# An attention and feed-forward kernel on one core: reciprocal ahead on VectorE, weight chunks over sixteen steps, transfers from SyncE, two banks for the down projection

## The chip, the cores and the metric

The kernel runs on one core of one Trainium2 chip. The metric is the device time of an execution in microseconds. Each core has TensorE (PE: matrix products into the eight banks of PSUM; PEld is its weight load), VectorE (DVE), ScalarE (ACT), GpSimd (POOL) and SyncE (SP, which here only issues transfers). Each engine executes its own instructions in the order of the program and waits at semaphores for the others.

## The reference

The input is x with 16 batches of 256 tokens and 256 features, all in float32. Two layers follow each other, each as x + layernorm(f(layernorm(x))):

```python
# attention, 16 heads of 128
q = (x @ Wq.T).reshape(b, n, 16, 128)
kv, kv_head, g = x @ Wkv.T, x @ Wkvh.T, x @ Wg.T
log_f_cumsum = cumsum(concat([0, log_sigmoid(g)]), axis=1)[:, :-1]
kv_head = cumsum(kv_head * exp(log_f_cumsum), axis=1)
k = einsum('bnd,bnh->bnhd', kv[..., :128], kv_head[..., :16])
v = einsum('bnd,bnh->bnhd', kv[..., 128:], kv_head[..., 16:])
q, k = rope(q), rope(k)
o = softmax(causal(q @ k / sqrt(128))) @ v;  out = o @ Wout.T
# feed forward
gate, up = split(x @ ternary_quant(w_gate_up).T)          # 2 x 1024
h = rms_norm(silu(gate) * up);  out = h @ ternary_quant(w_proj).T
```

ternary_quant works in bfloat16: a group of 64 weights has the scale mean(|w|), each weight is rounded to -1, 0 or 1 times it, and the result is w + (rounded - w).

## The kernel before

**Attention** goes over 16 batches, each in eight steps of two heads (a "pair"), 128 steps in all. The steps are software-pipelined by hand: the table `LAG` says how many steps after the projection of a pair (L725) a stage of it comes: cosine multiply on VectorE (`queries_cos`, L1273) and swap of halves on ScalarE (`swap`, L969) in the same step, sine multiply and addition on POOL one step later (L519, L528), the scores on TensorE (L742) and their maxima on VectorE (L1283) also one step later, softmax two (exponentials on ScalarE L981, `invert_sums`, the reciprocal of the sums, on VectorE L1299, `normalise` on POOL L550), transposition on TensorE three (L758) with its split into a high and a low part on ScalarE (L996) and VectorE (L1308), the product with the values four, the output projection five. Float32 products are three passes over high and low parts.

Work that comes once per batch lies in single steps by the tables `FRONT` (for the next batch) and `TAIL` (for the one before): layernorm statistics and normalisation of x (`stats_x`, `norm_x`, steps 0 and 1, VectorE, with `invert_x` on POOL), keys and gates (steps 3 and 4), decay and prefix sums (`decays` at the end of step 4, `coefs` and `sum_kv` in step 5), values (5 and 6), the copy of the attention's output and its layernorm (`copy_y` 5, `stats_y` 6, `norm_y` 7, with `invert_y` and `residual` on POOL).

The function `batch` of each engine writes the order within a step. On VectorE (L1460): statistics, norms, vh copy, key work, sums, then the reciprocal, the cosine multiply, `split_o`, the split and the maxima of each head, and at the end of the step `split_x`, `values_lo`, `decays` and the weight work. On POOL (L620): sine multiply, addition, `invert_x`, normalisation, scaling of the keys, the rest.

**Quantising the weights** takes six chunks, one in each turn of a loop of two batches (16 steps). The table `WSTEP` places its parts: load 0, cast 1 (ScalarE), sum 2, compare and decide 3, change 5, finish 6 (all VectorE, 128x1024 bfloat16), transposition on TensorE and copy on ScalarE 7, store 10. The six row blocks are first copied from input to a DRAM buffer by six transfers that ScalarE issues in step 4 of batch 0 (L1142).

**Transfers.** SyncE loads inputs, among them the first half of x (L402) ahead of the first store of the key sums (`store_kh`, L411); the stored sums of a pair are read back, spread over all partitions (`spread_kh`, L417), and `scale_keys` on POOL (L538) waits for them.

**The feed forward** goes over 16 units (a batch each) behind the attention: `up` in four parts (L823), the down projection `down` (L840) into the one bank `Y_BANK`, a sum of squares (L872), then the last layernorm, whose `norm_z` on ScalarE (L1074) reads the bank, and `add_x` on POOL. `down` of a unit waits until `norm_z` of the unit before has read the bank (L847).

## Time and profile before

| | us |
|---|---|
| median of 3 runs | 1161.29 (1160.11 to 1162.49) |
| the profiled execution | 1161.09 |
| its span, first to last instruction | 1159.3 |
| PE busy | 1076.3 (93%) |
| POOL busy | 914.9 (79%) |
| DVE busy | 874.5 (75%) |
| ACT busy | 845.0 (73%) |

The span has four stretches: the start and batch 0 up to about 84 us, six turns of the loop of 16 steps, each some 112 us long, three batches without weight work up to about 910 us, and the feed forward to the end. In a timeline a row has start, duration, engine, line, operation and tiles; brackets give the idle time of that engine just before the row, and which instruction's end ended it.

### The profile page before, as it was taken

Reading aid. Unit: us, or ns where it says so; the run is one execution under the profiler, and the core shown is the slowest. Engines: PE = TensorE matmul, PEld = TensorE weight load, DVE = VectorE, ACT = ScalarE, POOL = GpSimd, SP = SyncE. Lnnn points to the kernel's source line nnn. Section 1 sums busy time; section 2 is a strip of 40 time slices with the busy share of each in tenths; the row PEclk is TensorE's granted clock in tenths of the full one; section 3 lists DMA queues with packets and bytes.
Section 4 is the critical chain, followed back from the end, with each engine's and each line's share of the span. In section 5 each row is a group of like instructions: output and inputs, shape, how many; then the busy total and the mean of one; then the engine's idle time right before and its main releaser. Section 6 shows DMA issues by size and latency. Waiting matters only on the chain.

```text
span 1159.3 us, 26824 instructions
## 1 busy us (share of the span) xinstructions
PE 1076.3 (93%) x7990; PEld 1008.8 (87%) x7990; DVE 874.5 (75%) x2875; ACT 845.0 (73%) x2326; POOL 914.9 (79%) x845
## 2 busy tenths in 40 slices
PE   5799899989999999999899989999999899999996
PEld 4688898889888988898889888998988789999995
DVE  4578978897888779878987797878785656566563
ACT  2677777777777777787777777777777866666663
POOL 2687888797979797979798889888888647776774
PEclk8999999999999999999999999999999999999998
DMA  8260102010211111111011111111031000000000
GB/s 283 78 197 29 56 29 75 18 64 19 74 31 52 42 60 37 46 55 47 28 55 55 38 28 55 37 38 47 29 105 34 1 1 20 19 18 18 18 28 28
DMA packets 35192, 57.77 MB, mean 50 GB/s; under 512 B 3120, under 2 KB 15984, under 8 KB 34800
## 3 DMA queue, kind: packets, MB, share of 16 engines
q1 hardware_dynamic: 32912, 53.56, 14.9%
q10 hardware_dynamic: 2176, 3.15, 0.8%
q14 instruction: 78, 0.64, 0.2%
q8 instruction: 26, 0.43, 0.2%
HBM read 50.66 MB, written 9.18 MB: 52 GB/s over the span
## 4 chain that ended last, share of the span: by engine, by line
POOL 43%; issue 28%; PE 22%; ACT 3%; DVE 2%; DMA 1%; POOLq 1%; ACTq 0%; DVEq 0%; SPq 0%
POOL arena L526 13%; POOL arena L536 11%; POOL arena L547 9%; PE psum L835 8%; PE psum L852 6%; POOL arena L558 5%; PE psum L658 4%; POOL X L517 2%; ACT arena L1079 1%; PE psum L872 1%; POOL arena L503 1%; PE psum L753 1%; DVE pt_split L1318 1%; POOL arena L496 1%; PE psum L887 1%
## 5 line engine op out<-in xcount | busy, mean ns | idle before, releaser
L558 POOL TENSOR_TENSOR arena<-arena 128x768 f32<-128x768 f32 x128 | 188.2, 1470 | 106.7 <-DVE arena L1305 100.6
L526 POOL TENSOR_TENSOR arena<-arena,tables 128x512 f32<-128x512 f32 x128 | 174.4, 1363 | 17.5 <-ACT arena L979 17.5
L1318 DVE SCALAR_TENSOR_TENSOR pt_split<-psum,vh_col,pt_split 128x256 fp32r<-128x256 f32 (+1 forms) x512 | 187.3, 406 | 0.0
L753 PE MATMUL psum<-arena 128*128 128x256 f32 x512 | 157.6, 389 | 28.8 <-POOL arena L536 27.0
L536 POOL TENSOR_TENSOR arena<-arena 128x512 f32<-128x512 f32 x128 | 175.8, 1374 | 10.7 <-POOL arena L526 1.1
L990 ACT ACTIVATE arena<-arena 128x256 f32<-128x256 f32 x256 | 129.9, 507 | 74.4 <-DVE arena L1295 69.1
L547 POOL TENSOR_TENSOR arena<-arena 128x512 f32<-128x512 f32 x128 | 164.5, 1285 | 6.2 <-DMA arena<-kh_rows 6.2
L1280 DVE TENSOR_TENSOR arena<-psum,tables 128x512 f32<-128x512 f32 x128 | 86.1, 673 | 100.7 <-PE psum L658 95.2
L978 ACT ACTIVATE arena<-psum 64x512 f32<-64x512 f32 x128 | 76.1, 595 | 105.2 <-DVE arena L1280 105.1
L658 PE MATMUL psum<-wo_hi,o_hi 128*128 128x256 f32 x512 | 152.7, 298 | 0.0
L658 PE MATMUL psum<-xt_hi,wq_hi 128*128 128x256 f32 x512 | 146.9, 287 | 0.0
L658 PE MATMUL psum<-xt_lo,wq_hi 128*128 128x256 f32 x512 | 145.2, 284 | 0.0
L658 PE MATMUL psum<-xt_hi,wq_lo 128*128 128x256 f32 x512 | 145.0, 283 | 0.0
L658 PE MATMUL psum<-pt_split,vals_hi 128*128 128x512 f32 (+1 forms) x512 | 142.2, 359 | 2.8 <-DVE pt_split L1318 1.6
L658 PE MATMUL psum<-wo_hi,o_lo 128*128 128x256 f32 x512 | 144.2, 282 | 0.0
L658 PE MATMUL psum<-wo_lo,o_hi 128*128 128x256 f32 x512 | 143.7, 281 | 0.0
L835 PE MATMUL psum<-xt_hi,wq_hi 128*128 128x256 f32 x512 | 127.3, 288 | 0.4 <-DVE xt_lo L1452 0.3
L835 PE MATMUL psum<-xt_lo,wq_hi 128*128 128x256 f32 x512 | 124.3, 282 | 0.0
L1008 ACT ACTIVATE pt_split<-psum,vh_col 128x256 fp32r<-128x256 f32 x256 | 121.9, 476 | 0.6 <-PE psum L772 0.6
L753 PEld LDWEIGHTS psum<-arena 128*128 128x128 f32 x512 | 77.5, 190 | 39.1 <-issue 31.6
L564 POOL TENSOR_TENSOR wo_lo<-arena,wo_hi 128x512 fp32r<-128x512 f32 x64 | 89.1, 1400 | 25.9 <-ACT wo_hi L1057 25.9
L755 PEld LDWEIGHTS psum<-arena 128*128 128x128 f32 x512 | 97.2, 190 | 13.3
(161 smaller groups left out, 3511.5 us busy)
## 6 DMA issues: line engine op xcount, KB each, us to landing
arena<-kh_rows SPq DMA_DIRECT2D x128, 256.0 KB, 3.3
out<-spare SPq DMA_DIRECT2D x16, 256.0 KB, 2.1
arena<-w_rows SPq DMA_DIRECT2D x6, 512.0 KB, 4.3
X<-L_attn_Wout SPq DMA_DIRECT2D x1, 2048.0 KB, 14.8
X<-L_attn_x SPq DMA_DIRECT2D x1, 2048.0 KB, 9.5
w_rows<-L_ffn_w_gate_up ACTq DMA_DIRECT2D x4, 512.0 KB, 8.0
arena<-L_attn_Wq SPq DMA_DIRECT2D x1, 1536.0 KB, 10.4
X<-L_attn_x SPq DMA_DIRECT2D x1, 1536.0 KB, 15.7
```

What stands on the lines that cost most here:

```text
L526: nc.gpsimd.tensor_tensor(swap, swap, spread, ALU.mult).then_inc(q_sined, 1)
L536: nc.gpsimd.tensor_tensor(q_rot[p % 2], q_cos[p % 2], q_swap[p % 2], ALU.add).then_inc(q_roped, 1)
L547: nc.gpsimd.tensor_tensor(k_head[p % 2], keys[par].unsqueeze(1).to_broadcast([P, HP, N]), kh_all[p % 4], ALU.mult).then_inc(k_scaled, 1)
L558: nc.gpsimd.tensor_tensor(tb, tb, r.unsqueeze(3).to_broadcast([P, HP, 3, P]), ALU.mult).then_inc(p_ready, 1)
L564: nc.gpsimd.tensor_tensor(ht_lo[i][:, tiles, :], hid[i][:, tiles, :], ht_hi[i][:, tiles, :].bitcast(F32), ALU.subtract).then_inc(ht_lo_don ...
L658: last = nc.tensor.matmul(o, a, b, start=start and i == 0, stop=stop and i == len(passes) - 1, skip_group_check=skip)
L753: nc.tensor.matmul(sj[:, 0:2 * P], q[:, j, P:N], kt[:, j, :], start=True, stop=True, skip_group_check=True)
L755: nc.tensor.matmul(sj[:, 2 * P:3 * P], q[:, j, 0:P], kt[:, j, 0:P], start=False, stop=True, skip_group_check=True).then_inc(s_ready, 1)
L835: last = nc.tensor.matmul(bank[c % 2 * 2 + half][:, j * N:(j + 1) * N], wgu_t[:, k, col:col + P], part[:, k, :], start=n == 0 and j == 0, ...
L990: nc.scalar.activation(tb[:, j, 0:2 * P], tb[:, j, 0:2 * P], ACT.Exp, scale=-1.0, bias=nmax[p % 4][:, 2 * j:2 * j + 1], accum_out=rsum[p % ...
L1008: nc.scalar.activation(pt_hi[p % 2][:, j * N:(j + 1) * N], b[:, 0:N], ACT.Copy, scale=vh[:, 0, h:h + 1])
L1318: last = nc.vector.scalar_tensor_tensor(pt_lo[p % 2][:, o], b[:, i], vh[:, t, h:h + 1], pt_hi[p % 2][:, o].bitcast(F32), ALU.mult, ALU.sub ...
```

## The change

- `invert_sums` comes first in VectorE's step. After it: vh copy, the two new `bias_x` and `bias_y`, key work, sums, statistics, then most of the weight work, all ahead of the cosine multiply. Only "below" and "sign" of the weight work stay at the step's end.
- `norm_x` and `norm_y` move from VectorE to ScalarE as activations with scale and bias, behind `split_pt` and ahead of `swap`. VectorE makes the bias in one small instruction each.
- POOL's `invert_x` moves behind `normalise` and `scale_keys`.
- The weight chunk's steps are spread over the 16 steps. The comparison with -1 times the weight, a scalar_tensor_tensor, becomes a tensor_tensor with a negative threshold. The turned weights go to another buffer. TensorE's transposition is now in step 15.
- SyncE issues the row copies (one each in steps 1 to 6 of batch 0), the second half of x in step 7, the first half of x behind the first key sums, and the spreads two steps ahead of their step in its own order (with the same semaphore wait).
- The down projection alternates between banks 4 and 6 and waits for `norm_z` of two units before.

```diff
-WSTEP = dict(load=0, cast=1, sum=2, compare=3, decide=3, change=5, finish=6, turn=7, copy=7, store=10, stored=12)
+WSTEP = dict(cast=0, sum=1, scale=2, above=3, below=3, decide=7, sign=7, change=9, finish=11, turn=15, copy=15, store_chunk=15, next_load=13)
+        Z_BANK = [bank[4], bank[6]]
@@ SyncE
-            sp.dma_start(X[:, 2 * NT:half, :], tile_rows[:, 2 * NT:half, :]).then_inc(x_half, 16)
...
+            def spread_kh(g0, p):
+                at_least(sp, k_scaled, g - 3)
...
+                    spread_kh(g0, s + KH_LEAD)
+                    if isinstance(g0, int) and g0 == 0 and s >= ROWS_STEP and s < ROWS_STEP + CHUNKS:
...
+                        sp.dma_start(o, i_).then_inc(wt_rows, 16)
+                    if isinstance(g0, int) and g0 == 0 and s == PAIRS - 1:
+                        sp.wait_ge(w_turned, len(turns))
+                        sp.dma_start(w_stage.rearrange("p (t e) -> p t e", e=E), gu_rows[0]).then_inc(wt_in, 16)
+                        sp.dma_start(X[:, half:TILES, :], tile_rows[:, half:TILES, :]).then_inc(x_rest, 16)
             store_kh(0, 0)
+            for p in range(KH_LEAD):
+                spread_kh(0, p)
+            sp.dma_start(X[:, 2 * NT:half, :], tile_rows[:, 2 * NT:half, :]).then_inc(x_half, 16)
@@ POOL
-                    c0 = front_at(g0, s, "stats")
-                    if c0 is not None:
-                        invert_x(c0)
                     normalise(g0, s)
                     scale_keys(g0, par, s)
+                    c0 = front_at(g0, s, "stats")
+                    if c0 is not None:
+                        invert_x(c0)
@@ TensorE, down
-                        at_least(pe, z_norm, u * NT)
+                        at_least(pe, z_norm, (u - 1) * NT)
@@ ScalarE
+            def norm_x(c0):
+                act.wait_ge(ln1_biased, c0 + PAIRS)
+                for t in range(NT):
+                    nc.scalar.activation(xn[:, t, :], xs[:, t, :], ACT.Identity, bias=ln1_bias[:, t:t + 1],
+                                         scale=ln1_rstd[:, t:t + 1]).then_inc(ln1_done, PAIRS // NT)
...
                     split_pt(g0, par, s)
+                    c0 = front_at(g0, s, "norm")
+                    if c0 is not None:
+                        norm_x(c0)
+                    c0 = tail_at(g0, s, "norm")
+                    if c0 is not None:
+                        norm_y(c0)
                     swap(g0, s)
...
-                    if isinstance(g0, int) and g0 == 0 and s == ROWS_STEP:
...
-                            act.dma_start(o, i_).then_inc(wt_rows, 16)
@@ VectorE
+                nc.vector.scalar_tensor_tensor(ln1_bias, ln1_agg[:, :, 0], -1.0, ln1_rstd, ALU.mult, ALU.mult)\
...
-                    nc.vector.scalar_tensor_tensor(heads(w_other, GROUP), heads(w_bf, GROUP), -1.0, half, ALU.mult,
-                                                   ALU.is_gt).then_inc(wt_compared, ROUND)
+                    nc.vector.tensor_tensor(heads(w_other, GROUP), heads(w_bf, GROUP), spread_groups(w_below), ALU.is_lt)\
+                        .then_inc(wt_compared, ROUND)
...
+                    invert_sums(g0, s)
...
-                        norm_y(c0)
-                    invert_sums(g0, s)
+                    weights_sum(g0, par, s)
+                    weights_scale(g0, par, s)
+                    weights_above(g0, par, s)
+                    weights_decide(g0, par, s)
+                    weights_change(g0, par, s)
+                    weights_finish(g0, par, s)
                     queries_cos(g0, s)
```

## Rows read from the trace of the kernel before

**Rows 1.** The page, section 1: busy us, share, instructions.

```profile
PE 1076.3 (93%) x7990; PEld 1008.8 (87%) x7990; DVE 874.5 (75%) x2875; ACT 845.0 (73%) x2326; POOL 914.9 (79%) x845
```

**Rows 2.** Stretches: length, busy time of each engine, granted clock, DMA share, GB/s.

```profile
173.40:285.70 112.30, 106.32 (x778) 98.60 (x777) 94.18 (x326) 85.92 (x255) 95.87 (x78) 1.00 0.14 46
935.00:1150.00 215.00, 208.72 (x1708) 205.38 (x1707) 129.02 (x264) 141.33 (x268) 149.00 (x198) 0.99 0.06 19
```

**Rows 3.** Timeline of VectorE: a bare step (start, us, line, idle before).

```profile
876.98 0.20 DVE L1305 RECIPROCAL arena<-arena 128x8 f32<-128x8 f32 x1 [1.06 <-ACT arena L992]
...
878.50 0.69 DVE L1280 TENSOR_TENSOR arena<-psum,tables 128x512 f32<-128x512 f32 x1 [1.31 <-PE psum L658]
...
884.77 0.69 DVE L1280 TENSOR_TENSOR arena<-psum,tables 128x512 f32<-128x512 f32 x1 [1.30 <-PE psum L658]
```

**Rows 4.** Timeline of VectorE: cosine multiplies within sixteen steps.

```profile
195.53 0.69 DVE L1280 TENSOR_TENSOR arena<-psum,tables 128x512 f32<-128x512 f32 x1
...
215.62 0.69 DVE L1280 TENSOR_TENSOR arena<-psum,tables 128x512 f32<-128x512 f32 x1 [0.37 <-PE psum L658]
...
224.06 0.63 DVE L1280 TENSOR_TENSOR arena<-psum,tables 128x512 f32<-128x512 f32 x1
...
253.42 0.69 DVE L1280 TENSOR_TENSOR arena<-psum,tables 128x512 f32<-128x512 f32 x1 [1.30 <-PE psum L658]
...
294.80 0.69 DVE L1280 TENSOR_TENSOR arena<-psum,tables 128x512 f32<-128x512 f32 x1 [1.32 <-PE psum L658]
...
301.43 0.63 DVE L1280 TENSOR_TENSOR arena<-psum,tables 128x512 f32<-128x512 f32 x1
...
307.90 0.69 DVE L1280 TENSOR_TENSOR arena<-psum,tables 128x512 f32<-128x512 f32 x1
```

**Rows 5.** Groups of instructions, VectorE by form: busy us, mean ns, idle before.

```profile
L1194 DVE SCALAR_TENSOR_TENSOR arena<-X,arena 128x256 f32<-128x256 f32 x32 | 32.8, 1063 | 0.0
...
L1354 DVE SCALAR_TENSOR_TENSOR arena<-arena 128x1024 bf16<-128x1024 bf16 x6 | 13.9, 2311 | 0.0
...
L1373 DVE TENSOR_TENSOR arena<-arena 128x1024 bf16<-128x1024 bf16 x6 | 9.6, 1601 | 0.6
...
L1353 DVE TENSOR_TENSOR arena<-arena 128x1024 bf16<-128x1024 bf16 x6 | 7.3, 1220 | 0.0
...
L1362 DVE TENSOR_TENSOR arena<-arena 128x1024 bf16<-128x1024 bf16 x6 | 4.1, 691 | 0.6
```

**Rows 6.** Timeline of POOL: a drawn-out addition, a long wait.

```profile
219.39 2.23 POOL L536 TENSOR_TENSOR arena<-arena 128x512 f32<-128x512 f32 x1
...
288.71 1.47 POOL L558 TENSOR_TENSOR arena<-arena 128x768 f32<-128x768 f32 x1 [3.00 <-DVE arena L1305]
```

**Rows 7.** Timeline of TensorE: scores of a batch's first step.

```profile
308.39 0.69 PE L753 MATMUL psum<-arena 128*128 128x256 f32 x2 [0.76 <-POOL arena L536]
```

**Rows 8.** ScalarE: timeline, a wait in step 1; groups, one normalisation.

```profile
401.56 0.60 ACT L978 ACTIVATE arena<-psum 64x512 f32<-64x512 f32 x1 [1.29 <-DVE arena L1280]
...
L1071 ACT ACTIVATE arena<-X,arena 128x256 f32 (+1 forms) x32 | 17.3, 587 | 0.4 <-POOL arena L578 0.4
```

**Rows 9.** The start: timelines of POOL and ScalarE, one DMA issue.

```profile
27.55 1.28 POOL L547 TENSOR_TENSOR arena<-arena 128x512 f32<-128x512 f32 x1 [6.15 <-DMA arena<-kh_rows]
...
62.71 0.51 ACT L990 ACTIVATE arena<-arena 128x256 f32<-128x256 f32 x1 [5.18 <-issue]
...
X<-L_attn_x SPq DMA_DIRECT2D x1, 2048.0 KB, 9.5
```

**Rows 10.** Feed forward: timeline of TensorE, then VectorE.

```profile
1079.42 0.28 PE L835 MATMUL psum<-xt_lo,wq_hi 128*128 128x256 f32 x1
...
1079.89 0.39 PE L852 MATMUL psum<-wq_lo,wo_hi 128*128 128x256 f32 x1 [0.20 <-ACT arena L1079]
...
1144.91 0.36 PE L852 MATMUL psum<-wq_lo,wo_hi 128*128 128x256 f32 x1 [3.02 <-ACT arena L1079]
...
1145.27 1.67 DVE L1402 TENSOR_TENSOR arena<-arena 128x512 f32<-128x512 f32 x1
```

More of the change, by code:

```diff
@@ L151, in sandwich_kernel @@
         w_stage = carve(FF)
-        w_bf, w_signs, w_other, w_tern = (carve(FF // 2).bitcast(BF16) for _ in range(4))
+        w_words = [carve(FF // 2) for _ in range(4)]
+        w_bf, w_signs, w_other, w_tern = (a.bitcast(BF16) for a in w_words)
         keys_at = used[0]
@@ L262, in sandwich_kernel @@
         wt_rows, wt_in, wt_stored, wt_back = (sem(f"wt_{k}") for k in ("rows", "in", "stored", "back"))
[L263 to L264 removed]
+        wt_cast, wt_summed, wt_scaled, wt_above, wt_compared, wt_decided, wt_signed, wt_changed, wt_done, wt_turned, wt_copied = (
+            sem(f"wt_{k}") for k in ("cast", "summed", "scaled", "above", "compared", "decided", "signed", "changed", "done",
                                      "turned", "copied"))
@@ L939, in weight_hi, with norm_y @@
                 nc.scalar.activation(o, view(bank[b]), ACT.Copy).then_inc(w_hi_done, 1)
+            def norm_x(c0):
+                xs = x_tiles(c0)
+                act.wait_ge(ln1_biased, c0 + PAIRS)
+                at_least(act, xt_turned, c0)
+                for t in range(NT):
+                    nc.scalar.activation(xn[:, t, :], xs[:, t, :], ACT.Identity, bias=ln1_bias[:, t:t + 1],
+                                         scale=ln1_rstd[:, t:t + 1]).then_inc(ln1_done, PAIRS // NT)
+            def norm_y(c0):
+                act.wait_ge(ln2_biased, c0 + PAIRS)
+                act.wait_ge(x1_done, c0 + PAIRS)
+                for t in range(NT):
+                    nc.scalar.activation(y_norm[:, t, :], y_sb[:, t, :], ACT.Identity, bias=ln2_bias[:, t:t + 1],
+                                         scale=ln2_rstd[:, t:t + 1]).then_inc(ln2_done, PAIRS // NT)
             def split_x(c0, par):
@@ L1474, in batch @@
                         copy_vh(c0, par)
+                    c0 = front_at(g0, s, "norm")
+                    if c0 is not None:
+                        bias_x(c0)
+                    c0 = tail_at(g0, s, "norm")
+                    if c0 is not None:
+                        bias_y(c0)
                     c0 = front_at(g0, s, "decay")
```

167 lines of the change are left out of this document (81 added, 86 removed).

## Prediction

> **What bounds the kernel now.** I read the busy shares first: TensorE is busy 93% of the span, POOL 79%, VectorE 75%, ScalarE 73% [rows 1]. Then the stretches. In one turn of the loop (16 steps, 112.30 us) TensorE is busy for 106.32, so about 6 us are open in it; in the feed forward it is 208.72 of 215.00 [rows 2]. So no engine can be shortened into a large gain: what can be had is TensorE's waits and what makes them. The timeline of VectorE shows a bare step near the end of attention, with no work that comes once per batch: from one cosine multiply to the next 884.77 - 878.50 = 6.27 us. In it VectorE waits twice: 1.06 us for ScalarE's exponentials ahead of the reciprocal, and 1.31 us for TensorE ahead of the cosine multiply [rows 3]. I call the first the early gap and the second the late gap; their sum, 2.37 us, is what VectorE can take on in a step before the step grows. Work ahead of the reciprocal can use both gaps, work behind it only the late one.
>
> A batch with weight work takes 253.42 - 195.53 = 57.89 us, the next one without 307.90 - 253.42 = 54.48; eight bare steps would be 50.2 [rows 3, 4]. The chunk thus costs 3.4 us per turn. The dearest step holds both comparisons and "decide": 224.06 - 215.62 = 8.44 us [rows 4], with 1.22 + 2.31 + 0.69 = 4.22 us of them on VectorE [rows 5]. POOL has one long wait in each batch, 3.00 us in step 5, for a reciprocal that stands behind decay, coefficients and sums; it is behind from there on, and in the first step of the next batch TensorE's scores wait 0.76 us for POOL's addition [rows 6, 7].
>
> **The change part by part.** The sum is made against the profiled execution, 1161.09 us (span 1159.3), 0.2 under the median of the runs, 1161.29.
>
> *Reciprocal first.* In step 5 it no longer stands behind coefficients and sums. Of the 3.00 us wait some 2 go (1 remains from the decay work at the end of step 4, which stays ahead). POOL's addition then comes about 2 us sooner where TensorE waited 0.76 [rows 6, 7], so I take that wait as gone: 2 x 0.76 = 1.5 us per turn. Bounds: 0 (POOL falls behind again by other work) and 1.5. The wait that is moved forward holds what is queued behind it: vh copy, biases, keys, statistics and weight work start after ScalarE's exponentials. They have the late gap of 1.31 only. Statistics and key work, about 1 us or less, fit. The coefficients in step 5 did not fit before and are as long now.
>
> *Norms to ScalarE.* `norm_x` and `norm_y` leave VectorE, two instructions of 1063 ns each for x [rows 5]. Step 6 to 7, with `norm_y`, takes 301.43 - 294.80 = 6.63 us, 0.36 over the bare one [rows 3, 4]: 2 x 0.36 = 0.7 us per turn. The `norm_x` step is set by TensorE's extra work, so nothing more comes there. ScalarE gets twice 587 ns per norm, by its nearest activation. In step 1 it waited 1.29 us ahead of the swap, so `norm_x` is hidden [rows 8]; in step 7 the wait is smaller, and up to 0.9 us pushes the swap, the next exponentials and the reciprocal. POOL's queue is full there, so I take 0, with 0.5 per batch as the other end. TensorE's transposition of x waits for ScalarE instead of VectorE; it stands behind the scores, and I take 0. Moving `invert_x` behind two POOL operations delays its result by 2.7 us, which is wanted a step later: 0, and what loses that cover is a bias that comes late to ScalarE, ahead of the swap.
>
> *Weight work over 16 steps.* Sum, "above", "below" and "decide" fit their gaps: 1.22 each or less, against 1.06 and 1.31 [rows 3, 5]. The scalar_tensor_tensor of 2.31 us becomes a tensor_tensor that I price as its neighbour, 1.22 [rows 5]. What sticks out: "change" (0.7 to 1.6 us) in a late gap beside vh copy and bias, 0.35; "finish", alike, 0.3; "sign" 1.22 in the early gap of 1.06 ahead of statistics, 0.25; the transposition of the chunk, eight short matmuls on a TensorE that now has no time in hand in that step, with ScalarE's copy, 0.4. Sum 1.3 against 3.4 now: 2.1 us per turn, bounds 0.3 and 3.2. One row speaks about the price: POOL's addition at 219.39 takes 2.23 us while VectorE compares, where POOL's product of the same size takes 1.28, and "change" takes 1.60 where "decide", the same form, takes 0.69 [rows 5, 6, 9]. VectorE and POOL hold each other up.
> The Trainium skill (SBUF — State Buffer, "Who interferes with whom") says that a VectorE instruction with two SBUF inputs and a GpSimd instruction that reads SBUF block each other fully, whichever comes second. The trace agrees with it in the rows just named; by it "above" at the reciprocal's heels delays POOL's normalisation by its whole length.
>
> Per turn: 1.5 + 0.7 + 2.1 = 4.3 us, six turns: 26. The three batches behind them have only the first two terms, 1.1 + 1.1 and about 0.2 to 0.6 in the last, which has no next batch: 2.5.
>
> *The start.* POOL waits 6.15 us for the spread key sums, until 27.55 [rows 9], because their store and read-back share the DMA engines with the first half of x. With that behind them they come some 3 us sooner; TensorE's next projection then ends first, so I take 2 us. ScalarE loses 5.18 us to issuing six row copies ahead of its exponentials [rows 9]; the step around it is about 1.5 us longer than the same step later on, and that goes: 1.5. Added: the second half of x (2048 KB, 9.5 us to landing) is issued in step 7 instead of 4, and VectorE waits for it at the end of batch 0 [rows 9]. By my count it is issued at 64 behind one chunk and lands near 75, and VectorE gets there near 77: 0, but this is close, up to 3 us lost. Together 3.5, bounds 0 and 6.
> The Trainium skill (DMA: Bandwidth & Descriptors, "Queues, rings and completion order") says that an engine's transfers go through one ring per DMA engine in order, while different issuers take turns. No run here shows yet what one issuer makes of it; by it the spreads now stand behind 2 MB, where they took turns before.
>
> *Two banks.* In each unit TensorE waits for `norm_z` of the unit before; from the last product ahead of it to the first of `down` are 1079.89 - 1079.42 = 0.47 us, 0.20 of them a plain wait [rows 10], where the stage has a product every 215.00 / 1708 = 0.13 us [rows 2]: 0.34 x 12 = 4.1 us. In the last unit the wait is 3.02 us. Then the sum of squares on VectorE, ended at 1145.27 + 1.67 = 1146.94, is next late [rows 10]; without the wait the products would be done about then, not at 1150.3, so 3.3. Together 7.4, bounds 4 and 8.
>
> Sum: 26 + 2.5 + 3.5 + 7.4 = 39.4. 1161.1 - 39.4 = **1121.7**, the forecast.
>
> **The rivals.** *POOL takes over.* POOL is busy for 95.87 of a turn's 112.30 us and idle for 16.4 [rows 2]. "Above", "below", "sign", "change", "finish" and "decide" now start just when POOL may start, and in full they could add 3 x 1.22 + 3 x 0.69 = 5.7 us [rows 5] to it. If over half of its idle time, 9.4 us, stays because each step makes it wait for ScalarE and for the reciprocal, a turn is 95.9 + 5.7 + 9.4 = 111 us: 1.3 us gained instead of 4.3. The time is 1161.1 - 8 - 2 - 3.5 - 7.4 = **1140**. For it: the rows on mutual hold-up. Against: the idle time is there because POOL is early, and part of the 95.87 is hold-up by work that leaves VectorE.
>
> *Slower: the exponentials become late.* ScalarE takes the norms, the cast and the copy, and its exponentials free the reciprocal, which now stands ahead of everything. If they come later by the whole late gap, 1.3 us, in every step, all that stands behind the reciprocal lengthens its step; that is so in all steps but one, of which I take 4 as set by TensorE's own extra work: 11 x 1.2 = 13 us. A turn is then 112.3 - 4.3 + 13 = 121 us, and with start and feed forward gained 1161 + 52 - 11 = **1202**; the break-even lies where the delay exceeds about 0.7 us in most steps. For it: ScalarE rises from 85.92 us by 4.7 of 112 [rows 2, 8]. Against: 19% of its time stays free, and the waits recur in each bare step.
>
> *It doesn't do what it says.* The reciprocal's place is without effect, since POOL is not the last to arrive: the 1.5 us per turn stay, and only the rest comes: 1121.7 + 6 x 1.5 + 1.1 = **1132**, within the range.
>
> **How the numbers follow.** Forecast and the last rival: 0.76 (0.64 and 0.12), with an own range of 1108 to 1133. POOL takes over: 0.15. Slower: 0.05. The rest, 0.04: the gains of attention are eaten almost exactly (0.02) or it goes below 1107 (0.02). Low: the upper bounds, 3.2 + 1.5 + 0.7 = 5.4 per turn, 3, 6 and 8, give 1161 - 49 = 1112, and the uncertain loss to mutual hold-up that moving the norms takes off VectorE lets me go to 1107. High: 1140 and a little, 1142. A change of 0.2% (2.3 us) is about what a measurement of this kernel can tell from none: faster 0.93, same 0.02, slower 0.05.
>
> **What would show it.** A turn of the loop of about 108 us; POOL's wait for the reciprocal in step 5 near 1 us; no wait of scores for POOL in the first step of a batch; steps 3 and 4 no longer above 7.6 us; no 5 us hole on ScalarE near 60; down products 0.13 us behind their neighbours and the last unit's wait gone. I am wrong if cosine multiplies follow weight instructions with no wait for TensorE in many steps, if POOL has no idle time left, or if VectorE waits for the second half of x at the end of batch 0.

## The result and the profile after

| | kernel before | changed kernel |
|---|---|---|
| median us | 1161.84 (1160.11 to 1162.49, 4 runs) | 1143.94 (1142.95 to 1145.52, 4 runs) |
| ratio | | 0.9849, 95% interval 0.9832 to 0.9867 |
| span of the profiled execution | 1159.3 | 1142.0 |

The change is faster by 1.5%, 17.9 us; 39.4 were forecast, and 1143.94 lies just above the range. The busy shares, a turn of the loop and the feed forward, to be set against [rows 1, 2]:

```profile
PE 1069.9 (94%) x7990; PEld 1006.2 (88%) x7990; DVE 830.6 (73%) x2850; ACT 882.0 (77%) x2390; POOL 933.3 (82%) x845
```

```profile
192.75:303.46 110.71, 105.60 (x780) 98.38 (x780) 87.99 (x324) 90.56 (x263) 98.60 (x79) 1.00 0.15 46
923.00:1133.00 210.00, 206.50 (x1707) 203.43 (x1706) 127.23 (x263) 142.39 (x270) 148.78 (x198) 1.00 0.05 18
```

VectorE lost 44 us of work, ScalarE got 37, as planned. But POOL, which got no work at all, is busy 18 us longer. The cosine multiplies on VectorE's timeline give the steps (start, us, line, idle before), as in [rows 4]:

```profile
82.37 0.69 DVE L1303 TENSOR_TENSOR arena<-psum,tables 128x512 f32<-128x512 f32 x1 [0.35 <-PE psum L673]
...
192.75 0.69 DVE L1303 TENSOR_TENSOR arena<-psum,tables 128x512 f32<-128x512 f32 x1
200.63 0.67 DVE L1303 TENSOR_TENSOR arena<-psum,tables 128x512 f32<-128x512 f32 x1
...
213.17 0.69 DVE L1303 TENSOR_TENSOR arena<-psum,tables 128x512 f32<-128x512 f32 x1
220.76 0.67 DVE L1303 TENSOR_TENSOR arena<-psum,tables 128x512 f32<-128x512 f32 x1
228.66 0.65 DVE L1303 TENSOR_TENSOR arena<-psum,tables 128x512 f32<-128x512 f32 x1
...
295.60 0.69 DVE L1303 TENSOR_TENSOR arena<-psum,tables 128x512 f32<-128x512 f32 x1 [1.17 <-PE psum L673]
...
744.75 0.66 DVE L1303 TENSOR_TENSOR arena<-psum,tables 128x512 f32<-128x512 f32 x1
```

The multiply before the loop's first batch starts at 82.37 where it started at 83.63: 1.3 us from the start (3.5 forecast). From there to the end of the sixth turn it is 662.4 us, before 673.2: 10.8 us, 1.8 a turn (26 and 4.3 forecast). The three later batches gave 0.3 (2.5), the feed forward 4.9 (7.4). Nine tenths of the miss of 22 us are in the attention. The next table, read off the same rows of every kernel's trace, has the steps of one turn, the second, that differ (in the mean of all six turns it is 112.2 us before and 110.4 in the changed kernel); "a" is the half with steps 0 to 7, "b" the one with 8 to 15, and an entry is the time from one cosine multiply to the next. A bare step is 6.27 [rows 3]. In the three kernels on top all weight work is in half "a".

| kernel | a: 0→1 | 3→4 | 4→5 | 6→7 | 7→8 | b: 8→9 | 11→12 | 12→13 | 14→15 | 15→0 | turn |
|---|---|---|---|---|---|---|---|---|---|---|---|
| before | 7.47 | 8.44 | 8.10 | 7.52 | 6.22 | 7.58 | 7.32 | 7.58 | 6.63 | 6.47 | 112.4 |
| before_recip_first | 7.04 | 9.62 | 7.90 | 7.62 | 6.27 | 8.12 | 7.59 | 7.89 | 6.91 | 6.97 | 114.9 |
| before_norms_on_act | 7.25 | 8.46 | 8.10 | 6.87 | 6.78 | 7.04 | 7.30 | 7.58 | 6.30 | 6.37 | 111.0 |
| changed | 7.88 | 7.59 | 7.90 | 6.28 | 6.62 | 7.16 | 7.59 | 7.90 | 6.27 | 7.86 | 110.7 |
| recip_back | 7.61 | 7.29 | 7.58 | 6.30 | 6.66 | 8.29 | 7.33 | 7.58 | 6.30 | 7.15 | 109.6 |
| small_first | 7.03 | 7.29 | 7.90 | 6.28 | 6.70 | 7.17 | 7.29 | 7.90 | 6.28 | 7.62 | 109.2 |
| norms_back | 9.55 | 7.58 | 7.89 | 8.76 | 7.80 | 8.75 | 7.58 | 7.89 | 8.14 | 6.57 | 118.2 |
| all_keys_first | 7.03 | 7.33 | 7.58 | 6.29 | 6.74 | 7.29 | 7.13 | 7.58 | 6.27 | 6.88 | 108.4 |

The steps not shown are 6.2 to 6.7 us, but for 5→6 of the three kernels on top (7.5). Steps 11→12 and 12→13 have the same work in both kernels, 7.32 and 7.58 us before, 7.59 and 7.90 after, as 3→4 and 4→5. The timelines of VectorE and POOL show why, here in 3→4 and 4→5:

```profile
218.94 0.20 DVE L1328 RECIPROCAL arena<-arena 128x8 f32<-128x8 f32 x1 [0.92 <-ACT arena L1024]
...
219.39 1.44 DVE L1239 TENSOR_SCALAR arena<-arena 32x256 f32<-32x256 f32 x1
...
219.22 1.47 POOL L573 TENSOR_TENSOR arena<-arena 128x768 f32<-128x768 f32 x1
...
226.24 0.68 DVE L1250 TENSOR_TENSOR_SCAN arena<-arena,ones 32x256 f32<-32x256 f32 x1
...
227.63 1.10 DVE L1262 TENSOR_TENSOR_SCAN arena<-ones,arena 32x256 f32<-32x256 f32 x1 [0.20 <-DVE arena L1256]
...
226.28 1.91 POOL L573 TENSOR_TENSOR arena<-arena 128x768 f32<-128x768 f32 x1 [0.89 <-DVE arena L1328]
```

The reciprocal releases POOL's normalisation (L573), which starts at 219.22. The gate's addition (L1239), queued right behind the reciprocal, needs 0.27 us by itself; it starts at 219.39 and ends only when the normalisation does. One step on the same happens to the second scan (1.10 us, 0.68 by itself), and this time the normalisation is drawn out as well, to 1.91: the first scan (L1250) had started 0.04 us ahead of it.

### The profile page after: what moved, and what is told of

It is laid out like the page before. It is cut to its first block, busy times and chain, and to the rows that moved or that the text cites. A ratio compares the mean times of both kernels' runs of the same rounds, so it can differ in the third digit from the quotient of the medians.

```text
span 1142.0 us, 26842 instructions
## 1 busy us (share of the span) xinstructions
PE 1069.9 (94%) x7990; PEld 1006.2 (88%) x7990; DVE 830.6 (73%) x2850; ACT 882.0 (77%) x2390; POOL 933.3 (82%) x845
## 4 chain that ended last, share of the span: by engine, by line
PE 33%; POOL 21%; issue 20%; DVE 16%; ACT 8%; DVEq 1%; POOLq 0%; ACTq 0%; DMA 0%
PE psum L673 14%; PE psum L850 8%; POOL arena L551 6%; DVE pt_split L1341 6%; POOL arena L541 5%; POOL arena L562 5%; PE psum L867 3%; POOL arena L573 2%; PE psum L768 2%; ACT arena L1022 1%; PE psum L785 1%; ACT arena L1024 1%; DVE arena L1318 1%; DVE o_lo L1350 1%; DVE arena L1303 1%
## 5 line engine op out<-in xcount | busy, mean ns | idle before, releaser
L573 POOL TENSOR_TENSOR arena<-arena 128x768 f32<-128x768 f32 x128 | 208.9, 1632 | 60.7 <-DVE arena L1328 60.1
L541 POOL TENSOR_TENSOR arena<-arena,tables 128x512 f32<-128x512 f32 x128 | 164.1, 1282 | 34.4 <-ACT arena L1011 30.9
L551 POOL TENSOR_TENSOR arena<-arena 128x512 f32<-128x512 f32 x128 | 175.4, 1370 | 10.6 <-POOL arena L541 1.1
L562 POOL TENSOR_TENSOR arena<-arena 128x512 f32<-128x512 f32 x128 | 170.3, 1330 | 8.4 <-DMA arena<-kh_rows 8.4
L768 PE MATMUL psum<-arena 128*128 128x256 f32 x512 | 154.5, 383 | 4.3 <-POOL arena L551 4.3
L785 PE MATMUL psum<-ident,arena 128*128 128x128 f32 x256 | 75.3, 294 | 39.3 <-DVE pt_split L1341 35.3
L1328 DVE RECIPROCAL arena<-arena 128x8 f32<-128x8 f32 x128 | 24.8, 194 | 117.9 <-ACT arena L1024 117.9
```

What stands on the lines that cost most here:

```text
L541: nc.gpsimd.tensor_tensor(swap, swap, spread, ALU.mult).then_inc(q_sined, 1)
L551: nc.gpsimd.tensor_tensor(q_rot[p % 2], q_cos[p % 2], q_swap[p % 2], ALU.add).then_inc(q_roped, 1)
L562: nc.gpsimd.tensor_tensor(k_head[p % 2], keys[par].unsqueeze(1).to_broadcast([P, HP, N]), kh_all[p % 4], ALU.mult).then_inc(k_scaled, 1)
L573: nc.gpsimd.tensor_tensor(tb, tb, r.unsqueeze(3).to_broadcast([P, HP, 3, P]), ALU.mult).then_inc(p_ready, 1)
L768: nc.tensor.matmul(sj[:, 0:2 * P], q[:, j, P:N], kt[:, j, :], start=True, stop=True, skip_group_check=True)
```

## The experiments

Theory A: VectorE and POOL hold each other up, and the reciprocal at the head of the step puts all of VectorE's small work beside the normalisation that it releases. Its main rivals: the reciprocal's place does nothing (B); ScalarE's new load ate the gain (C). Each other letter is explained in the expectation in which it stands.

**recip_back** moves one line of the changed kernel.

```
                 for s in range(steps):
-                    invert_sums(g0, s)
...
+                    invert_sums(g0, s)
                     queries_cos(g0, s)
```

> The changed kernel with one line moved: the reciprocal of the sums (invert_sums) stands directly ahead of the cosine multiply again, behind the keys, biases, statistics and the weight work that now stands there. Theory A, hold-up: in the changed kernel the reciprocal at the head of the step starts the normalisation on POOL just as VectorE works off its small operations, and the two hold each other up (L1239 1.44 us where the kernel before had 0.27, L1262 1.10 where it had 0.68, L1221 1.11). With the reciprocal behind them these fall back to about 0.3, 0.7 and 0.2 us, step 3 to 4 comes back from 7.59 to about 7.3; but TensorE's score matmul waits for POOL's addition again, about 0.76 us in each of the first steps and as much again behind the weight work. Net 0.5 to 1.5 us a turn slower than the changed kernel: 1147 to 1153. Rival B, the place of the reciprocal does nothing: 1144 within 1. Rival C, ScalarE's load is what ate the gain: these three operations may get shorter, the time stays within 1 of 1144, and step 15 to 0 stays at 7.9.

Measured: 1135.46 us (1134.55 to 1136.40), 8.5 us *faster* than the changed kernel. The mechanism of A is there: 3→4 is 7.29, 4→5 is 7.58, and POOL's normalisation is back at its own length, as the groups of the page say (busy us, mean ns, idle before), changed kernel first, then this one:

```profile
L573 POOL TENSOR_TENSOR arena<-arena 128x768 f32<-128x768 f32 x128 | 208.9, 1632 | 60.7 <-DVE arena L1328 60.1
```

```profile
L573 POOL TENSOR_TENSOR arena<-arena 128x768 f32<-128x768 f32 x128 | 188.3, 1471 | 100.4 <-DVE arena L1328 92.0 <-PE psum L770 8.4
```

My net had the wrong sign, though: all three expectations are missed. I still charged the waits of the scores for POOL in full, and left out that the transposition's wait for VectorE would fall. The waits of TensorE (us in total, times, longest) over the whole run, changed kernel first, then this one:

```profile
PE psum L785 <- DVE pt_split L1341: 35.3, 97, 1.7
...
PE psum L768 <- POOL arena L551: 4.3, 7, 0.7
```

```profile
PE psum L768 <- POOL arena L551: 12.7, 15, 1.4
PE psum L785 <- DVE pt_split L1341: 11.5, 45, 1.7
```

**before_recip_first** is the same line moved the other way in the kernel before, from ahead of the cosine multiply to the head of the step.

> The kernel before with the reciprocal of the sums alone moved to the head of the step. Theory A, hold-up: the 0.76 us waits of the scores go (1.5 us a turn), but norm_x and norm_y, the gate's addition and the sum scan now stand behind the reciprocal beside the normalisation; each is lengthened by 0.4 to 1.2 us, so the time is 1155 to 1163, near the kernel before. Rival B, the place does nothing: 1162 within 1, and those operations keep their lengths. The prediction's own sum (no hold-up): 1.5 us in each of six turns and 0.76 in each of three later batches, 11 us: 1151.

Measured: 1184.45 us (1182.86 to 1186.84), ratio 1.0205 (1.0179 to 1.0231), 22.6 us slower than before. All three were too low. The waits of TensorE (us in total, times, longest), kernel before and then this one:

```profile
PE psum L753 <- POOL arena L536: 27.0, 34, 1.9
PE psum L770 <- DVE pt_split L1318: 18.0, 54, 1.1
```

```profile
PE psum L770 <- DVE pt_split L1318: 56.9, 117, 2.1
...
PE psum L753 <- POOL arena L536: 1.9, 2, 1.6
```

The prediction was right that the early reciprocal removes the scores' wait for POOL's addition: 27.0 to 1.9 us. It did not see what takes its place: the transposition of the probabilities waits 56.9 us in place of 18.0 for `pt_split`, because VectorE reaches the cosine multiply late. In the table: 11→12 up by 0.27, 12→13 by 0.31, 3→4 9.62 for 8.44. In 3→4 it is again the gate's addition behind the reciprocal, 1.49 us long:

```profile
228.42 1.49 DVE L1213 TENSOR_SCALAR arena<-arena 32x256 f32<-32x256 f32 x1
```

**norms_back** puts `norm_x` and `norm_y` of the changed kernel back on VectorE, behind the reciprocal. VectorE's part:

```
                     c0 = front_at(g0, s, "norm")
                     if c0 is not None:
-                        bias_x(c0)
+                        norm_x(c0)
                     c0 = tail_at(g0, s, "norm")
                     if c0 is not None:
                         bias_y(c0)
+                        norm_y(c0)
```

> The changed kernel with both layer normalisations of the loop (norm_x, norm_y) back on VectorE, in the places where their biases stand now, behind the reciprocal. Theory A, hold-up: they run beside the normalisation on POOL, 1.9 us and more for each pair; steps 0 to 1 and 6 to 7 grow by 0.7 to 1.3 us each, four a turn, and step 15 to 0 gives back about 1.2 and step 7 to 0 0.3: 1.5 to 3.5 us a turn slower, 1153 to 1165. Rival C, ScalarE's load: with 2.2 us a batch taken off ScalarE the exponentials come in time, step 15 to 0 falls from 7.86 to 6.3, and the sum is 1136 to 1143.

Measured: 1198.56 us (1196.78 to 1200.23), 54.6 slower than the changed kernel; C is out, and A's price was too low by half or more. Steps with a norm behind the reciprocal grow by 1.6 to 2.5 us (6→7 is 8.76 for 6.28). One instruction of `norm_y` takes 1544 ns in the mean, one of `norm_x` 1413; in the kernel before they took 1138 and 1063 (the second is in [rows 5]), and in before_recip_first, where the order alone is changed, 1180 and 1294. Step 15→0 falls from 7.86 to 6.57, nearly the 6.3 that C says of that one step; the other steps cost far more than it gives.

```profile
L1309 DVE SCALAR_TENSOR_TENSOR arena<-arena 128x256 f32<-128x256 f32 x32 | 48.2, 1544 | 0.0
L1227 DVE SCALAR_TENSOR_TENSOR arena<-X,arena 128x256 f32<-128x256 f32 x30 | 41.2, 1413 | 0.0
```

**before_norms_on_act** has the two norms alone on ScalarE in the kernel before, the reciprocal in its old place.

> The kernel before with the two normalisations alone moved to ScalarE (bias_x and bias_y on VectorE in their old places). Theory A says that the change's gain came from here, not from the reciprocal: VectorE's 1.9 us of step 6 to 7 go (7.52 and 6.63 to 6.3), step 0 to 1 falls from 7.5 to about 7.0, and step 7 to 0 grows by 0.4 to 0.6 in the batch whose ScalarE copies the chunk: 2 to 2.7 us a turn and 0.8 to 1 in each later batch: 1143 to 1149. Rival C, ScalarE's load: the exponentials of the next step come late by as much as VectorE saves, both 1.1 us long on ScalarE: 1157 to 1163. The prediction's terms for it (0.7 a turn for norm_y, none for norm_x): 1156.

Measured: 1153.3 us (1153.22 to 1154.82), 9.2 faster than the kernel before it was run beside (1162.48; ratio 0.9931, 0.9910 to 0.9952). The turn of the table gained 1.35 us, the mean of six 1.2: 6→7 and 14→15 gave 0.65 and 0.33, 0→1 and 8→9 0.22 and 0.54, and 7→8, where ScalarE copies the chunk, took 0.56. Between my sizes for A and for the prediction. It gave back 1.5 us at the start, where one step of batch 0 grew from 8.3 to 10.9 us; I did not follow that. So the norms are worth 9 us with the reciprocal late and 55 with it early: the two parts of the change are not independent. The two pairs of kernels differ in the weight work as well, but the lengths just given say that a norm costs more on VectorE beside the normalisation.

**small_first** leaves the reciprocal early and takes the small work out of its wake: `bias_x`, `bias_y` and `keys_cos` go ahead of it, where VectorE waits for the exponentials anyway.

```
                 for s in range(steps):
+                    (the calls of bias_x, bias_y and keys_cos)
                     invert_sums(g0, s)
-                    (the calls of bias_x, bias_y and keys_cos)
```

> The changed kernel with the biases (bias_x, bias_y) and the keys' cosine multiply with the gate's addition (keys_cos) moved ahead of the reciprocal, into the 1.0 us in which VectorE waits for the exponentials. Theory A, hold-up: the gate's addition is back at 0.3 us and step 3 to 4 falls from 7.59 to 6.6 to 7.0, the bias of step 1 from 1.11 to 0.2 us and step 0 to 1 of the first half from 7.88 to about 7.0; 1.5 to 2 us a turn and 0.6 in each later batch: 1131 to 1136. Rival B and C (the hold-up is no cost on the path; the reciprocal only comes up to 0.5 us later): 1144 to 1148.

Measured: 1134.27 us (1133.07 to 1135.45), 9.7 faster than the changed kernel, as A says. 0→1 is 7.03, as expected; 3→4 is 7.29, where 6.6 to 7.0 was expected.

**gap_filled** moves the scans with their multiply (`coefs`, `weigh_kv`, `sum_kv`) and the statistics (`stats_x`, `stats_y` with their gathering) ahead of the reciprocal in the same way.

> The changed kernel with all small work of the late gap but the copy of vh and the weight work put ahead of the reciprocal: biases, keys_cos, the scans and their multiply (coefs, weigh_kv, sum_kv), and the statistics with their gathering. Theory A, hold-up (the reciprocal starts POOL's normalisation beside VectorE's small work, so what stands ahead of it runs undisturbed, in the time in which VectorE waits for the exponentials): beyond what small_first gained, step 4 to 5 falls from 7.90 to 7.58 in every batch, and step 15 to 0 from 7.64 to about 7.15 since the statistics run before the late exponentials end; 108.0 to 108.5 us a turn: 1125 to 1130. Rival D, what counts is that the reciprocal comes early for POOL, and the keys' move helped for another reason: the scans ahead of it, 1.9 us, delay the normalisation, the score waits for POOL again, and the time goes back to 1136 to 1142.

Measured: 1134.78 us (1134.23 to 1136.08): no gain over small_first, between the ranges of A and D. 4→5 is 7.58, as A says, but 8→9 went from 7.17 to 8.27. There the sign of the weights, at the end of step 7, now meets POOL's sine, not its addition, and they hold each other up one operation earlier; so the addition and the scores behind it come later:

```profile
240.37 1.79 DVE L1410 TENSOR_TENSOR arena<-arena 128x1024 bf16<-128x1024 bf16 x1
...
241.04 2.27 POOL L541 TENSOR_TENSOR arena<-arena,tables 128x512 f32<-128x512 f32 x1
...
244.79 0.69 PE L768 MATMUL psum<-arena 128*128 128x256 f32 x2 [1.39 <-POOL arena L551]
```

**small_normalise** changes nothing on VectorE. It cuts what the reciprocal releases to 8 of every 128 columns, and leaves the rest of the softmax undivided.

```
-  tensor_tensor(tb, tb, r...to_broadcast([P, HP, 3, P]), ALU.mult)
+  tensor_tensor(tb[:, :, :, 0:8], tb[:, :, :, 0:8], r...to_broadcast([P, HP, 3, 8]), ALU.mult)
```

> The changed kernel with POOL's normalisation cut to the first 8 of each 128 columns: most of the softmax is left undivided, so that the operation that the reciprocal starts is short; nothing on VectorE moves. Theory A, hold-up between the two engines: VectorE's operations behind the reciprocal lose their neighbour: the gate's addition falls from 1.44 to 0.3 us, the second scan from 1.10 to 0.7, the bias of step 1 from 1.11 to at most 0.4; step 3 to 4 falls from 7.59 to 7.3, 4 to 5 from 7.90 to 7.58; 1132 to 1138. Rival H, the operations are long since they stand right behind the reciprocal on VectorE (a wait or a start cost of their own): they keep 1.44, 1.10 and 1.11 us, and steps 3 to 4 and 4 to 5 keep 7.59 and 7.90.

Measured: one run at 1139.44 us, 1.4 above A's bound. The timelines of VectorE and POOL where the changed kernel had 1.44 and 1.47:

```profile
217.70 0.27 DVE L1240 TENSOR_SCALAR arena<-arena 32x256 f32<-32x256 f32 x1
...
217.53 0.27 POOL L573 TENSOR_TENSOR arena<-arena 128x48 f32<-128x48 f32 x1 [1.39 <-DVE arena L1329]
...
225.65 1.13 DVE L1263 TENSOR_TENSOR_SCAN arena<-ones,arena 32x256 f32<-32x256 f32 x1 [0.20 <-DVE arena L1257]
...
226.19 1.12 POOL L518 TENSOR_TENSOR arena<-arena 128x256 f32<-128x256 f32 x1
```

3→4 is 7.29, 4→5 7.93. The gate's addition takes 0.27 us in the same place behind the reciprocal: the neighbour was the cause, not the place (H is out for it). The second scan keeps 1.13, against A's number but not against its mechanism: POOL has moved on and now adds the keys' rotation beside it (1.12 us where that takes 0.72 to 0.74 in the changed kernel). The bias of step 1 keeps 0.98 us where A had at most 0.4, and 0→1 is 7.73; there POOL's scaling of the keys, 0.33 us ahead of the bias, has come into the normalisation's place. Which operation is hit depends on which ones overlap.
The Trainium skill (SBUF — State Buffer, "Who interferes with whom") says that a VectorE instruction with two SBUF inputs, or a `tensor_scalar` in its two-port mode, and a GpSimd instruction that reads SBUF exclude each other, and that "issue order, not op shape, decides who blocks". These rows agree, by their lengths 0.27 and 1.44, 1.47 and 1.91; which mode the addition ran in no row shows.

**one_bank** takes the second bank away.

```
-        Z_BANK = [bank[4], bank[6]]
+        Z_BANK = [bank[6], bank[6]]
...
-                        at_least(pe, z_norm, (u - 1) * NT)
+                        at_least(pe, z_norm, u * NT)
```

> The changed kernel with one down-projection bank again (both of Z_BANK the same bank, the wait on z_norm of the unit before as it was). The prediction's terms: 0.34 in each of 12 units and 3.3 in the last ones, 7.4 us: 1151. Theory A for the units (the wait for z_norm was replaced by the wait of the next unit's first gate matmul for VectorE's x2_lo, so a unit of the loop gains only 0.05): 0.6 + 3.3, 1148, and the units of its loop at 13.2 to 13.35. Rival E (the banks bring nothing, the end's gain is from elsewhere): 1144.

Measured: 1147.40 us (1147.23 to 1151.10), 3.5 slower than the changed kernel. From one sum of squares on TensorE to the next a pair of units in the loop takes 26.5 us with one bank and with two; the last two intervals are 13.23 + 13.30 with one and 12.84 + 10.00 with two. So 3.7 us come in the last two intervals. From the last cosine multiply of the attention to the end of the span it is 249.4 us in the kernel before and with one bank, 244.6 with two: the second bank is worth 4.9 us by this stretch and 3.5 by the medians. In the profiled executions the attention, the same program in both, ran 1.4 us shorter with one bank (its last cosine multiply starts at 896.07 for 897.45), and that hides the rest.

**split_first** goes for what holds the loop's units in its place, the first gate product's wait for `xt_lo`: x2's rounding (ScalarE) and splitting (VectorE) go ahead of the third chunk. VectorE's part:

```
+                    nc.vector.tensor_tensor(x2_lo[i]...)
                     multiply(*at, 2)
-                    nc.vector.tensor_tensor(x2_lo[i]...)
```

> The changed kernel with, in each unit of the feed forward, the rounding and the splitting of the next unit's x2 put ahead of the third chunk's silu and multiply, on ScalarE and on VectorE. Theory A (with two banks a unit's limit is the wait of the first gate matmul for xt_lo, 0.2 to 0.5 us): that wait goes and a unit falls from 13.2 to 12.85 to 13.0, 12 to 15 units: 1139 to 1141. Rival F (the unit's length is set by the third chunk's silu and multiply, or by POOL, and they now come 0.5 us later): 1144 to 1148.

Measured: 1142.76 us (1142.41 to 1142.95), units as long as before. TensorE's timeline, changed kernel first, then this one:

```profile
1009.71 0.38 PE L850 MATMUL psum<-xt_hi,wq_hi 128*128 128x256 f32 x1 [0.22 <-DVE xt_lo L1497]
```

```profile
1006.55 0.66 PE L902 MATMUL psum<-ident,arena 128*128 128x128 f32 x4 [0.25 <-ACT arena L1103]
```

One wait went, another came: x2's transposition now waits for ScalarE's `norm_x2`, which stands behind a rounding that waits for VectorE.

**keys_first_norm_first** puts `norm_x2` ahead of that rounding too, and in the attention has the biases, keys and scans ahead of the reciprocal. ScalarE's part:

```
                     activate(*at, 1)
+                    norm_x2(*at)
                     high_hidden(*at, 1)
-                    norm_x2(*at)
```

> Two parts, one in each stage, read by their own stretches. Attention: the changed kernel with the biases, keys_cos and the scans ahead of the reciprocal, the statistics left behind it (the better half of gap_filled). Theory A: step 4 to 5 7.58 in every batch, step 0 to 1 7.05 and 7.15 as in small_first, since the bias no longer waits for POOL behind an early statistic and the sign no longer meets the next step's sine: 108.5 us a turn, 4 to 5 us below small_first. Rival D (the reciprocal should be early for POOL): no faster than small_first. Feed forward: split_first with ScalarE's norm_x2 put ahead of the second chunk's rounding. Theory A (split_first took the wait of the first gate matmul away and put in its place a wait of x2's transposition for norm_x2, 0.25 to 0.4 us a unit): both go, the loop's units fall from 13.25 to 12.85 to 12.95, 3.5 to 5 us in all. Rival F (the loop itself or POOL sets the unit): 13.2. Both by A: 1124 to 1127; both by the rivals: 1134 to 1136.

Measured: 1134.05 us (1133.13 to 1134.71). The feed forward does what A says, each unit now 12.84 us by the sums of squares:

```profile
996.68 0.95 PE L887 MATMUL psum<-ones,arena 128*128 128x1 f32 x8
1009.52 0.95 PE L887 MATMUL psum<-ones,arena 128*128 128x1 f32 x8
1022.36 0.95 PE L887 MATMUL psum<-ones,arena 128*128 128x1 f32 x8
```

It took three waits, one behind the other (bank, `xt_lo`, `norm_x2`), to get the 0.4 us a unit. The attention was a miss: 110.3 us a turn where I expected 108.5. 8→9 is 8.25, by the collision that gap_filled has, and 15→0 is 8.25, where ScalarE now stands idle for 1.48 us ahead of the first exponential of the next turn, for 1.05 in the changed kernel.

**copy_on_vector** takes the copy of the turned chunk from ScalarE to the end of VectorE's step 15, from keys_first_norm_first.

```
-                nc.scalar.activation(w_turned_bf.bitcast(BF16), F_BANK.bitcast(BF16), ACT.Copy)
+                nc.vector.tensor_copy(w_turned_bf.bitcast(BF16), F_BANK.bitcast(BF16))
```

> keys_first_norm_first with the copy of the turned chunk (step 15) taken from ScalarE and put at the end of VectorE's step. Theory A for step 15 to 0 (7.6 to 7.9 us where the other half has 6.6: norm_y 1.1 us and the chunk's copy 1.0 us both stand on ScalarE ahead of the exponentials that start the next turn): that step falls to 6.6 to 6.9, 0.8 to 1.1 us a turn: 5 to 6 us below keys_first_norm_first. Rival I, the 0.8 to 1.0 us in which ScalarE stands at the end of the loop's turn comes whatever it did before: 0 to 1 us. Rival J: VectorE's copy, which now stands ahead of its reciprocal, takes the same time there: 0 to 2 us below.

Measured: 1127.55 us (1127.14 to 1128.62), 6.5 less: A. 15→0 falls from 8.25 to 6.88. In the changed kernel ScalarE has, in step 15 (timelines of ScalarE, then VectorE):

```profile
295.88 1.12 ACT L970 ACTIVATE arena<-arena 128x256 f32<-128x256 f32 x2
...
298.25 1.02 ACT L1064 ACTIVATE arena<-psum 128x1024 bf16<-128x1024 bf16 x1
300.33 0.51 ACT L1022 ACTIVATE arena<-arena 128x256 f32<-128x256 f32 x1 [1.05 <-DVE arena L1318]
...
302.24 0.20 DVE L1328 RECIPROCAL arena<-arena 128x8 f32<-128x8 f32 x1 [2.91 <-ACT arena L1024]
```

`norm_y`, the chunk's copy and 1.05 us at the end of the loop's turn stand in a row ahead of the exponentials, and the reciprocal waits 2.91 us in place of 1.06 [rows 3]. (The profile puts the 1.05 down to VectorE's maxima, but the last of these had ended at 299.33.) On VectorE the same copy takes 0.68 us, in the time in which it waits. Not all of the 1.4 us of the step is the copy's, though: ScalarE's idle time at that place also fell, from 1.48 to 1.00 us, and why is open.

**sign_later** is keys_first_norm_first with the weight work's later steps moved.

```
-WSTEP = dict(... decide=7, sign=7, change=9, finish=11 ...)
+WSTEP = dict(... decide=7, sign=10, change=11, finish=14 ...)
```

> keys_first_norm_first with the sign of the weights moved from step 7 to step 10, the change from 9 to 11 and the finish from 11 to 14. Theory A, hold-up: the sign on VectorE (1.8 to 2.0 us where it has 1.2 alone) and POOL's sine or addition (2.1 to 2.3 for 1.3) lengthen each other in step 7, which has the residual on POOL as well, and the scores of the next step wait for it; moved to a step with room on both, step 7 to 0 of the first half falls from 6.68 to 6.3 and step 0 to 1 of the second from 7.15 to 7.05, step 10 to 11 grows by at most 0.1: 2 to 3 us below keys_first_norm_first. Rival K: the sign costs as much wherever it stands, since POOL is busy in every step: within 1 us of keys_first_norm_first.

Measured: 1130.65 us (1129.92 to 1132.03), 3.4 less, A's direction and a little more than its size: 8→9 from 8.25 to 7.27, with 10→11 and 13→14 longer by 0.17 and 0.43.

**all_keys_first, all_small_first, all_recip_back** have the sign late, the copy on VectorE and the feed forward's new order, and differ in the reciprocal alone: behind keys and scans, ahead of the scans, behind everything.

> copy_on_vector and sign_later together: biases, keys_cos and scans ahead of the reciprocal. Theory A, hold-up: sign_later took 0.6 us from a turn (step 8 to 9 from 8.25 to 7.27, steps 10 to 11 and 13 to 14 0.2 and 0.4 longer) and copy_on_vector 1.4 (step 15 to 0 from 8.25 to 6.88); the two are in different steps and add: 108.3 to 108.5 us a turn, 1123 to 1126. If they don't add, one of the two waits stands in for the other: 1127.

> The same with the scans behind the reciprocal (biases and keys_cos ahead of it). Theory A, hold-up: step 4 to 5 is 7.90 in place of 7.58 (the second scan, 1.1 us beside POOL), 0.32 in each of 15 batches and nothing else: 4 to 5 us slower than all_keys_first, 1127 to 1131. Rival D, the early reciprocal has a worth of its own: up to 3 us faster than all_keys_first.

> The same with the reciprocal directly ahead of the cosine multiply, behind everything. Theory A, hold-up: VectorE's work is undisturbed here too, and only the waits for POOL's addition in the first step of a batch are back (step 0 to 1 7.6 in place of 7.03 in the first half, 0.57 a turn): 2 to 4 us slower than all_keys_first, 1126 to 1129. The prediction's reading (the place of the reciprocal is worth 1.5 us a turn and more behind the weight work): 9 to 15 us slower, 1133 to 1139. Rival B, no worth at all: within 1 of all_keys_first.

Measured: 1123.73, 1124.16 and 1123.75 us (ratios 0.9678, 0.9677 and 0.9668, each within 0.0025). The two parts add, and the first kernel came as expected. The other two are a miss of A's sizes: once the worst collisions are gone the reciprocal's place is worth nothing that these runs could tell, either way (B). The scan beside POOL still costs all_small_first its 0.32 us in 4→5, as much again in 12→13 and 0.3 in 13→14, and it has them back in 7→8 (6.31 for 6.74), 8→9 (7.04 for 7.29) and 15→0 (6.50 for 6.88). Waits of TensorE, in that order:

```profile
PE psum L785 <- DVE pt_split L1337: 11.3, 46, 1.7
PE psum L768 <- POOL arena L551: 8.5, 22, 0.7
```

```profile
PE psum L785 <- DVE pt_split L1337: 25.8, 89, 1.7
...
PE psum L768 <- POOL arena L551: 0.7, 1, 0.7
```

```profile
PE psum L768 <- POOL arena L551: 10.0, 24, 0.7
PE psum L785 <- DVE pt_split L1337: 10.0, 40, 1.7
```

The waits for POOL and for VectorE trade places at a sum of 20 to 27 us; in all_keys_first TensorE is busy for 105.86 of a turn's 108.41:

```profile
188.86:297.27 108.41, 105.86 (x777) 98.56 (x777) 88.98 (x323) 89.23 (x263) 95.91 (x79) 1.00 0.15 47
```

These are the fastest kernels of this study, 3.2% under the kernel before and 1.8% under the changed one.

## Why the prediction was wrong

- **Reciprocal first, +1.5 us a turn: the step that failed, in its sign.** By the mean of six turns the way from the kernel before to the changed one is 112.2 us, 111.0 (before_norms_on_act), 109.5 (recip_back), 110.4: the norms gave 1.2, the weight work with all that goes with it 1.6, the reciprocal -0.9. The terms were 0.7, 2.1 and 1.5, so this one makes 2.4 of the 2.5 us missed in a turn. What it was to release came: POOL's wait in step 5 fell from 3.00 us to 0.89, the waits of the scores for POOL from 27.0 to 4.3. But the waits of the transposition for VectorE rose from 18.0 to 35.3. The sentence that failed is "statistics and key work, about 1 us or less, fit": they fit by lengths measured beside an idle or earlier POOL. Released ahead of them, the normalisation stretches the gate's addition from 0.27 to 1.44, the second scan from 0.68 to 1.10, the bias of step 1 to 1.11. Step 15→0 is another matter: the exponentials come late there, the statistics stand behind them, and the 0.7 us that go when the reciprocal moves back (7.15) are a matter of order, not of hold-up. One line moved costs 8.5 us here and 22.6 in the kernel before. The rows on mutual hold-up stood in the prediction, for the weight work alone; the rival charged it to POOL, while most of it fell on VectorE's late gap.
- **Norms, +0.7: too small.** before_norms_on_act has 1.2 a turn in the mean. The step with `norm_x`, which I held to be set by TensorE, gave 0.2 to 0.5 too. Beside an early reciprocal they are worth far more.
- **Weight work, +2.1: about 1.6.** By before_norms_on_act against recip_back, which differ by POOL's order and SyncE's as well. The comparison priced at 1.22 took 1.22. "Change" and "finish" cost 0.3 each or less, as priced, and took 0.68 and 0.65 us; "sign", priced at 1.22, took 1.94 beside POOL. The chunk's transposition and copy, priced at 0.4, stand in 15→0, which is 1.6 over a bare step where the other half's 7→8 is 0.35 over: `norm_y` in that same step and the end of the loop's turn had used up ScalarE's time.
- **Later batches, +2.5: 0.3.** Both terms were read into batches that had little to give: 53.9 to 54.0 us long before, and 53.2 to 53.7 in the fastest kernels here.
- **Start, +3.5: 1.3.** The key sums came 3.4 us sooner (POOL's first product at 24.17 for 27.55 [rows 9]) and ScalarE's hole of 5.18 us is gone. Step 3→4 of batch 0 gave 1.3 back, 9.50 us for 8.23. Hold-up shows in two rows of that batch, the gate's addition with 1.45 us for 0.27 and the second scan with 1.19 for 0.68. The rest is open: one_bank and split_first, with the same attention, start the loop's first cosine multiply at 81.59 and 81.22 where the changed kernel has 82.37, so about 1 us can't be told from chance here. gap_filled has 8.23 in 3→4 and starts at 80.09, 3.5 us sooner than before, but 0.9 of its 2.3 us ahead of the changed kernel is there at batch 0's first cosine multiply (19.00 for 19.91). That the term was right but for hold-up is likely, not shown. The second half of x, taken to land near 75, landed near 80.0, 0.9 us before VectorE's statistics on it at 80.91: no wait, as priced, but closer than thought. And the spreads did not take turns with it before: SyncE issued that half itself at 50.99 and the next spread at 51.41. In neither kernel does an engine wait for a spread after the first.
- **Two banks, +7.4: 4.9 by the feed forward's own stretch, 3.5 by the medians.** The last unit's 3.3 was right, down to what is next late, `sum_squares` on VectorE:

```profile
1132.91 1.05 PE L887 MATMUL psum<-ones,arena 128*128 128x1 f32 x8 [1.02 <-DVE arena L1447]
```

  The 0.34 in each of 12 units was not: with the bank's wait gone the next unit waits for `xt_lo`, then for `norm_x2`. I had not asked what was next late inside the loop.
- **Slower rival:** no sign of it outside 15→0. **"Doesn't do what it says"** took the reciprocal to be worth 0, and it was worth less. **"POOL takes over"** had the size nearly right, 1140, by luck: it charged POOL, and recip_back, with POOL's early start taken away, is faster.

## What to carry to other kernels

Before an operation is moved to release another engine sooner, list what it releases and what then stands beside it: on VectorE and POOL an operation's length is not its own. Fill the wait ahead of the releasing operation with small work, not the time behind it, or leave the releasing operation behind the small work: with the collisions gone both came to the same time here. And when a wait is taken away, look for the second latest arrival at the same instruction and in the same round of the loop; a term is only as large as the distance to it.

## What the runs showed of the hardware

- A VectorE addition of 32x256 takes 0.27 us, beside a POOL operation of 1.47 us it takes 1.44, and when that one is cut to 0.27 us it takes 0.27 again. Even a bias of 128x2 took 1.11 beside it.
- The same copy of a bank, 128x1024 bf16, takes 1.02 us on ScalarE and 0.68 on VectorE.
- Between its last instruction of one turn of the loop and its first of the next, whose input is there, ScalarE stands idle: 0.85 to 1.06 us in the changed kernel, 1.42 to 1.63 in keys_first_norm_first, 0.47 to 0.54 in norms_back. What sets the length is open. It shows in the time only where ScalarE has no other time in hand.
